# Variance as squares on ScalarE, a two-piece output projection and a new order in a hybrid block of two attentions and two feed-forwards

## The reference

```python
x = x + attn_a(layernorm(x))     # one head of 128
x = x + ffn(layernorm(x))        # 512 -> 512, weight dequantised from 4 bits
x = x + attn_b(layernorm(x))     # 32 heads of 16, rotary, causal
x = x + ffn(layernorm(x))        # the same weights again

def layernorm(x, eps=1e-5):
    return (x - mean(x)) / sqrt(var(x) + eps)
def attn_b(x):
    q, k, v = x @ wq, x @ wk, x @ wv          # 512x512 each
    q, k = rotary(q), rotary(k)
    return softmax(causal(q @ k.T / 4)) @ v @ wo
```

## Time and profile before

| | us |
|---|---|
| median of three runs | 279.03 |
| profiled execution, own time | 280.3 |
| its span, first to last instruction | 278.3 |
| TensorE busy | 259.2 |
| VectorE busy | 227.9 |
| GpSimd busy | 180.8 |
| ScalarE busy | 145.0 |

### The profile page before, as it was taken

The page is one execution under the profiler, slowest core; times in us unless marked ns, Lnnn a source line. Parts: engine busy times, 40 slices in busy tenths (PEclk is TensorE's granted clock), DMA queues, the critical chain, the costliest instruction groups (busy, mean ns, idle before and its releaser), DMA issues.

```text
span 278.3 us, 6590 instructions
## 1 busy us (share of the span) xinstructions
PE 259.2 (93%) x2358; PEld 212.6 (76%) x2358; DVE 227.9 (82%) x390; ACT 145.0 (52%) x231; POOL 180.8 (65%) x233
## 2 busy tenths in 40 slices
PE   7489999999999999899899999899999799997984
PEld 2389887797979888687887987877778667785642
DVE  3772869879699999989998999988999888838656
ACT  3768885743465354548225459336265464273140
POOL 5556989999783947746589777477649630573060
PEclk9999999999999999999999999999999999999999
DMA  7995090202454445315423633043454431121002
GB/s 221 324 389 199 1 246 22 75 2 84 144 151 124 126 132 148 96 58 149 115 71 104 189 104 103 24 131 102 124 160 114 132 91 50 41 78 40 0 15 98
DMA packets 50903, 31.85 MB, mean 114 GB/s; under 512 B 5368, under 2 KB 46008, under 8 KB 50872
## 3 DMA queue, kind: packets, MB, share of 16 engines
q1 hardware_dynamic: 50872, 31.44, 37.2%
HBM read 22.91 MB, written 8.39 MB: 112 GB/s over the span
## 4 chain that ended last, share of the span: by engine, by line
PE 73%; SPq 8%; DMA 7%; DVE 6%; issue 3%; ACT 1%; POOL 1%; DVEq 0%; POOLq 0%
PE psum L838 12%; PE psum L839 11%; PE psum L840 11%; SPq L467 6%; PE psum L1001 5%; PE psum L922 5%; PE psum L923 5%; PE psum L864 4%; PE psum L987 4%; PE psum L966 4%; PE psum L912 3%; DMA QK<-mrow 2%; PE psum L964 2%; PE psum L989 2%; DMA QK<-qk_parts 2%
## 5 line engine op out<-in xcount | busy, mean ns | idle before, releaser
L556 POOL TENSOR_SCALAR_AFFINE_SELECT E<-E 128x512 f32<-128x512 f32 x64 | 40.1, 652 | 37.1 <-ACT E L682 37.0
L682 ACT ACTIVATE E<-psum 128x1536 f32<-128x1536 f32 x32 | 46.4, 1450 | 31.9 <-PE psum L989 27.5
L794 DVE TENSOR_REDUCE nmax<-psum 128x4 f32<-128x512 f32 (+1 forms) x64 | 59.5, 943 | 2.5 <-PE psum L966 2.3
L838 PE MATMUL psum<-XT_lo,wb_hi 128*128 128x256 f32 x128 | 38.6, 301 | 0.0
L585 ACT ACTIVATE XN<-X,offset,rstd 128x512 f32<-128x512 f32 x32 | 25.5, 806 | 20.5 <-POOL offset L518 20.5
L839 PE MATMUL psum<-XT_hi,wb_lo 128*128 128x256 f32 x128 | 36.1, 282 | 0.0
L840 PE MATMUL psum<-XT_hi,wb_hi 128*128 128x256 f32 x128 | 36.1, 282 | 0.0
L563 ACT ACTIVATE parts<-SH 128x512 bf16<-128x512 f32 x32 | 19.8, 626 | 27.8 <-POOL SH L545 14.3
L838 PE MATMUL psum<-wb_lo,XT_hi 128*128 128x256 f32 (+1 forms) x96 | 31.9, 333 | 0.5 <-DVE inv_o L808 0.3
L966 PE MATMUL psum<-QK 128*128 128x128 bf16 x256 | 29.7, 220 | 1.4 <-DMA QK<-qk_parts 1.4
L840 PE MATMUL psum<-wb_hi,XT_hi 128*128 128x256 f32 (+1 forms) x96 | 30.6, 318 | 0.0
(11 more groups left out here) (101 smaller groups left out, 676.6 us busy)
## 6 DMA issues: line engine op xcount, KB each, us to landing
QK<-qk_parts SPq DMA_DIRECT2D x192, 64.0 KB
qk_parts<-parts SPq DMA_DIRECT2D x16, 384.0 KB, 2.8
X<-L_attn_a_x SPq DMA_DIRECT2D x8, 256.0 KB, 5.7
out<-X SPq DMA_DIRECT2D x8, 256.0 KB, 2.1
wb_raw<-L_attn_b_wk SPq DMA_DIRECT2D x1, 1024.0 KB, 9.0
wb_raw<-L_attn_b_wq SPq DMA_DIRECT2D x1, 1024.0 KB, 11.4
wb_raw<-L_attn_b_wv SPq DMA_DIRECT2D x1, 1024.0 KB, 12.4
QK<-mask_rows SPq DMA_DIRECT2D x8, 128.0 KB
```

The source lines that it names most:

```text
L556: last = nc.gpsimd.affine_select(out=e, in_=e, compare_op=ALU.is_ge, fill=0.0, base=0, pattern=[[0, GH], [1, P]], channel_multiplier=-1)
L682: nc.scalar.activation(E[:, n % 2], bank(3, 3), ACT.Exp, scale=float(HD) ** -0.5).then_inc(done[k], 1)
L794: nc.vector.tensor_reduce(nmax[:, u % 2, g::NG, t], (bank(1, 2) if t else bank(0)).rearrange("p (h k) -> p h k", h=GH), AX, ALU.max, negat ...
L838: nc.tensor.matmul(out_, stat[0], mov[1], start=first, stop=False)
```

## The change

- `LN` stays for the eight tiles of the first norm and the last batch's two tiles of the fourth. For the other 22 tiles the addition that makes X (`WD`, `FD`, `OD`) also sums its row (`accum_out`), and a new ScalarE step `SQ` makes the squares of sum minus 512 x, with their sum. `RS` scales either kind of statistics; two of its operations on a tensor of constants become operations with immediates, and the first two do not wait for each other.
- `WO` goes in two pieces, the first three 128s of the contraction (nine matmuls) and the last one (three); `DH` and `DL` too.
- For the last batch's last feed-forward `F`, `FD` and `OS` go in two halves of 256 columns.
- `NX` divides in place and `NB` reads it with strides; the buffer `TN` is gone.
- Several waits of TensorE that an earlier wait covers are gone.
- `PLAN` is written in a new order, with three `KP` steps (14, 5 and 5 matmuls) in place of four (14, 4, 5 and 7).

The diff without the list and without the dropped waits:

```diff
+PIECES = (slice(0, KT - 1), slice(KT - 1, KT))
+        def row_sums(s, b, t):
+            return {} if ("LN", s, b, t) in nth else {"accum_out": mv[:, (s - 1) * B + b, t, 0:1]}
...
+                    if ("SQ", s, b, 0) in nth:
+                        pool.wait_ge(done["SQ"], last_of(*[("SQ", s, b, t) for t in range(NT)[ts]]))
+                        one, square = 1.0 / C, float(C) ** -3
+                    else:
+                        pool.wait_ge(done["LN"], last_of(*[("LN", s, b, t) for t in range(NT)[ts]]))
+                        one, square = 1.0, 1.0
+                    nc.gpsimd.tensor_scalar(mv[:, sl, ts, 0], mv[:, sl, ts, 0], -one, None, ALU.mult).then_inc(pool_link, 1)
+                    links[0] += 1
+                    link(nc.gpsimd.tensor_scalar(mv[:, sl, ts, 1], mv[:, sl, ts, 1], square, EPS, ALU.mult, ALU.add))
...
+                elif k == "SQ":
+                    s, b, t = st[1:]
+                    act.wait_ge(done[made_x(s, b, t)[0]], upto(*made_x(s, b, t)))
+                    if nth[st]:
+                        act.wait_ge(done["SQ"], nth[st])
+                    moments = mv[:, (s - 1) * B + b, t]
+                    nc.scalar.activation(squares[:], X[:, b, t], ACT.Square, bias=moments[:, 0:1], scale=-float(C),
+                                         accum_out=moments[:, 1:2]).then_inc(done[k], 1)
...
-                    act.wait_ge(done["NB"], last_of(*[("NB", KT * b + m) for m in range(KT)]))
+                    act.wait_ge(done["NB"], last_of(*[("NB", KT * b + m) for m in range(KT)[PIECES[piece]]]))
...
-                    nc.vector.tensor_tensor(X[:, b, t], X[:, b, t], prod, ALU.add).then_inc(done[k], 1)
+                    if s == 2:
+                        last = nc.vector.scalar_tensor_tensor(X[:, b, t], X[:, b, t], 1.0, prod, ALU.mult, ALU.add,
+                                                              **row_sums(3, b, t))
+                    else:
+                        last = nc.vector.tensor_tensor(X[:, b, t, cols], X[:, b, t, cols], prod, ALU.add)
+                    last.then_inc(done[k], 1)
...
-                    nc.vector.tensor_tensor(X[:, b, t], X[:, b, t], bank(bank_of["WO", b, t]), ALU.add
-                                            ).then_inc(done[k], 1)
+                    nc.vector.scalar_tensor_tensor(X[:, b, t], X[:, b, t], 1.0, bank(bank_of["WO", b, t, 0]), ALU.mult,
+                                                   ALU.add, **row_sums(4, b, t)).then_inc(done[k], 1)
...
-                    nc.vector.tensor_tensor(TN[:].rearrange("p (i g d) -> p i g d", g=NG, d=HD), tr[:, :, :, 0:HD],
+                    nc.vector.tensor_tensor(tr, tr,
...
-                    nc.vector.transpose(O[:, m], TN[:]).then_inc(done[k], 1)
+                    nc.vector.transpose(O[:, m], TR[:].rearrange("p (g i d) -> p i g d", g=NG, d=2 * HD)[:, :, :, 0:HD]
+                                        ).then_inc(done[k], 1)
...
-                    for kt in range(KT):
+                    for kt in range(KT)[PIECES[piece]]:
                         last = three_pass(ps, [xt[:, slot, kt, tok] for xt in (XT_hi, XT_lo)],
                                           [w[:, 3, kt] for w in (wb_hi, wb_lo)], kt == 0, kt == KT - 1)
```

More of the change, by code:

```diff
@@ L239, in bank_turns @@
             continue
-        if k not in READ_BY or (k in PAIRS and st[2]):
+        if k not in READ_BY or (k in PAIRS and st[2]) or (k == "WO" and st[3]):
             continue
@@ L388, in xt_half, with output_part, columns @@
             return xt[:, xt_of[st], :, t * P:(t + 1) * P]
+        def output_part(xt, b, t, piece):
+            return xt[:, xt_of["DH", b, t, piece], PIECES[piece], t * P:(t + 1) * P]
+        def columns(st, at):
+            return slice(st[at] * S, (st[at] + 1) * S) if len(st) > at else slice(0, C)
         part_of = (slice(0, 2 * DA), slice(2 * DA, 3 * DA))
@@ L477, in _ @@
                 elif k == "OS":
-                    b, t = st[1:]
-                    sp.wait_ge(done["FD"], upto("FD", 4, b, t))
-                    sp.dma_start(out_v[b, t], X[:, b, t]).then_inc(out_done, 16)
-            sp.wait_ge(out_done, 16 * B * NT)
+                    b, t = st[1:3]
+                    sp.wait_ge(done["FD"], upto("FD", 4, *st[1:]))
+                    sp.dma_start(out_v[b, t][:, columns(st, 3)], X[:, b, t, columns(st, 3)]).then_inc(out_done, 16)
+            sp.wait_ge(out_done, 16 * count["OS"])
         @block.gpsimd
@@ L751, in _ @@
                     nc.vector.scalar_tensor_tensor(X[:, b, t], bank(bank_of["WA", b, t]), inv_a[:, b % 2, t:t + 1],
-                                                   X[:, b, t], ALU.mult, ALU.add).then_inc(done[k], 1)
+                                                   X[:, b, t], ALU.mult, ALU.add, **row_sums(2, b, t)).then_inc(done[k], 1)
                 elif k == "FS":
@@ L822, in _ @@
                     dve.wait_ge(done["NX"], upto("NX", u))
-                    if m == 0 and b:
-                        dve.wait_ge(done["DL"], last_of(*[("DL", b - 1, t) for t in range(NT)]))
-                    nc.vector.transpose(O[:, m], TN[:]).then_inc(done[k], 1)
+                    if m in (0, KT - 1) and b:
+                        dve.wait_ge(done["DL"], last_of(*[("DL", b - 1, t, int(m > 0)) for t in range(NT)]))
+                    nc.vector.transpose(O[:, m], TR[:].rearrange("p (g i d) -> p i g d", g=NG, d=2 * HD)[:, :, :, 0:HD]
+                                        ).then_inc(done[k], 1)
         @block.tensor
@@ L858, in _ @@
                 elif k == "T":
-                    pe.wait_ge(consts_ready, 2)
                     no = ("NO", *st[1:])
@@ L919, in _ @@
                         pe.wait_ge(done["WC"], KT)
-                    ps = take(st)
+                    ps = take(st)[:, 0:cols.stop - cols.start]
                     for kt in range(KT):
-                        nc.tensor.matmul(ps, XT_lo[:, slot, kt, tok], wf[:, kt], start=kt == 0, stop=False)
-                        last = nc.tensor.matmul(ps, XT_hi[:, slot, kt, tok], wf[:, kt], start=False, stop=kt == KT - 1)
+                        nc.tensor.matmul(ps, XT_lo[:, slot, kt, tok], wf[:, kt, cols], start=kt == 0, stop=False)
+                        last = nc.tensor.matmul(ps, XT_hi[:, slot, kt, tok], wf[:, kt, cols], start=False,
+                                                stop=kt == KT - 1)
                     last.then_inc(done[k], 1)
@@ L995, in _ @@
                     pe.wait_ge(done["MK"], upto("MK", u, g))
-                    pe.wait_ge(done["VV"], upto("VV", u // 2))
+                    if u % 2 == 0 and g == 0:
+                        pe.wait_ge(done["VV"], upto("VV", u // 2))
                     ps = (bank(bank_of["PV", u, 0]) if g else take(st))[:, g * S:(g + 1) * S]
```

86 lines of the change are left out of this document (42 added, 44 removed), and 257 rows, old and new, of the table PLAN.

## The result

The kernel after takes 278.06 us, median of 22 runs (276.35 to 280.67), against 279.6 us for the kernel before in the same comparison (22 runs, 278.41 to 280.96). The ratio is 0.993, with a 95% interval of 0.991 to 0.995: 2.0 us faster (0.7% of 279.6; the medians lie 1.5 us apart), where 6.5 us were forecast. Two of the 22 runs, at 280.51 and 280.67 us, are more than 1.5% above the fastest and are left out of the ratio. The profiled execution took 278.1 us, with a span of 276.4 us, against 280.3 and 278.3 before.

The account below looks back on a forecast made before the run. TensorE was taken to bound the long middle, chains of dependent steps the head and tail. Gains of 1.4 + 3.0 + 0.8 + 1.3 = 6.5 us against the median 279.03 gave 272.5 us, range 269.0 to 278.5.

Parts of the forecast that it names:

- The middle: 30 to 250 us: with VectorE relieved and the new order, 3.0 of TensorE's 6.1 us idle go; bounds nothing and 6.1.
- the middle gives nothing: Rival: TensorE's middle waits are for DMAs and their issuing queue, not VectorE; only 3.5 us won, 275.5 us; chance 0.12.
- The other half of the argument: Middle, unit 12: 60 matmuls instead of 36 stand between transposed maxima (MT) and the product needing them (ST).
- The head: Start to about 29 us: first QK matmul 2.8 us sooner, at about 11.9; net gain 1.4 us, bounds 0 and 2.8.
- The end of the heads: 250 to 256.3 us: F 4,1,1 before the last units and moved transposes win 0.8 of 1.2 us idle.
- The tail: Last 22 us: projection in pieces and halved last feed-forward end 1.3 us sooner; fillers spend the early win; bounds 0.5 and 3.5.
- The prices: Assumed instruction costs: squares with accumulator read 0.99 us each, row-sum additions 0.1 us more each, halved copies some 0.1 us.
- The lower bound of the relief: VectorE's work was to fall by 10 to 19 us, 14 taken; the lower bound is the 10.
- ScalarE as the relay: Rival: squares waiting in ScalarE's in-order queue hold exponentials and copies behind them, up to 281 to 282 us; chance 0.16.
- seven exposed squares: In the ScalarE rival: each exposed square costs 0.99 us or more; from 7 of 22 the whole gain is gone.
- only eats the gain: Milder part of the ScalarE relay rival: 277.6 to 280.4 us; chance 0.07 of its 0.16.
- The clock: Rival in the tail: clock drops to 1.2 GHz, four half products (3.8 us) take twice as long, 276.3 us; chance 0.04.

Follow-up runs that it names:

- experiment 2: No statistics for 22 tiles: old order against the kernel before, 279.55 us, ratio 1.001; kernel after without its squares, 276.86 us, ratio 0.991.
- the relieved run, the run without statistics: Old order with no statistics for 22 tiles (constant variance), in-place division and row sums in, against the kernel before: 279.55 us, ratio 1.001.
- experiment 1: Parts alone: new order with VectorE's statistics 285.72 us; squares in the old order 285.29 us; new tail in the old order 287.48 us.
- late pieces: Kernel after with both first pieces of the last batch copied and subtracted no earlier than the last piece: 285.51 us, ratio 1.021.
- both fillers: Kernel after plus ten filler matmuls in the head's pause and five in the tail's: 277.04 us, ratio 0.989.
- experiment 4: Kernel after with the last batch's first pieces late, 285.51 us, ratio 1.021; kernel after without the tail's ten fillers, 278.74 us, ratio 0.997.
- experiment 3: Old order with squares on ScalarE, one copy of transposed exponentials moved ahead of two squares: 284.19 us, ratio 1.015; unmoved 285.29 us.
- the run without fillers: Kernel after without the ten filler matmuls of the tail: 278.74 us, ratio 0.997.
- both fillers and both moves: Kernel after with fillers in its two longest pauses, plus TensorE work moved into two waits of the middle: 280.48 us, ratio 1.002.

## Why the forecast was wrong

Of the 6.5 us, 1.9 came in the spans. The missing 4.6 us are about 2.3 in the middle and 2.0 in the head.

**The middle (3.0 us forecast, 0.7 us less idle).** This is the step that failed first: that VectorE, at 192.6 of 220 us, delays what it hands on, so that half of TensorE's 6.1 us of idle time would go with its relief. In the old order the relief, without its price on ScalarE, is worth 0.0 us (ratio 1.001, experiment 2). A mean load told me that VectorE was late, but not where: at the longest wait of the old order the relief took nothing away, and VectorE is as full there as before (6.94 of 7.00 us). Issue and transfer, 4.1 us, take the rest. The rival "the middle gives nothing" (275.5 us) had this nearly right, though not its reason: the queue that issues was not in the way at 217 us, the two transfers of unit 12 were issued 0.07 us behind VectorE's result in the relieved run. The other half of the argument, the 60 matmuls between MT and ST of unit 12, did remove that wait; but 1.0 us for normalised rows, 0.8 for nmax and a wait of 1.3 for stacked parts (0.9 the longest before) stand in the new order. What the relief does is carry the new order (7.6 us, experiment 1), and that order only makes good what its own positions ask of VectorE.

**The head (1.4 us forecast).** The working was right to 0.2 us for the first product, and from there to 29 us the longest wait is indeed 0.3 us. It put at nothing what lies ahead of that product: one pause of 2.4 us, made of two of 1.5, since the second tile's transposes came earlier and the third normalisation did not. The pause costs nothing by the chain, but in the profiled execution the granted clock fell to 0.50 behind it, 1.46 us at QV, which eats the forecast's 1.4. An estimate of the whole from TensorE's busy time up to 30 us (23.59 before; 25.38 after, of which 1.46 are the fall and 0.91 the slower fillers at the start) has TensorE 0.6 us behind in work. By the same reckoning the executions with late pieces and with both fillers, which kept their clock, are 1.1 to 1.2 us ahead, so the term itself was near.

**The end of the heads (0.8 us forecast).** Idle time there is 0.56 us (6.30 - 5.74), 0.6 less than before. About right in size. But F 4,1,1 was not moved forward: it stood ahead of unit 13's PV and now stands behind unit 14's scores, so this busy time came into the stretch from the middle.

**The tail (1.3 us forecast, 1.3 measured).** Right, and with its parts: 3.67 us to the first addition for 3.6, the second tile's transposes 13.3 us behind VectorE's transposition as before, and the last addition's end 1.1 us nearer to it (274.16 - 255.73 = 18.43, before 275.89 - 256.36 = 19.53). Wrong was to call the fillers a loss (experiment 4).

**The prices.** Squares take 719 ns and 193 ns for their accumulator read, 0.91 us for the 0.99 taken. Additions with a row sum were bounded by 0 and 0.28 us and taken as 0.1. The addition itself costs nothing more (688 ns for 687), and there is a second instruction of 82 ns, as the Trainium skill, "VectorE: DVE Perf Modes", section "Two Vector instructions with no wait between them", says:

```profile
L803 DVE SCALAR_TENSOR_TENSOR X<-X,psum 128x512 f32<-128x512 f32 x8 | 5.5, 688 | 0.3
...
L803 DVE DVE_READ_ACCUMULATOR X<-X,psum 128x1 f32 x8 | 0.7, 82 | 0.0
```

Two pieces of a remainder take 627 and 467 ns for one of 769, so 0.33 us more a tile, where some 0.1 was taken; the two copies, 518 and 302 ns for 621, cost 0.20. The lower bound of the relief was added up wrong as well: its own terms give 9 us, not 10. The division in place looks cheaper by the mean, 421 ns for 641, but not by the median (min/median/max, before and after):

```profile
L816 DVE TENSOR_TENSOR TN<-TR,inv_o x16: 406/421/2492, 112.2 to 257.4; 128x256 f32<-128x256 f32 x16
```

```profile
L855 DVE TENSOR_TENSOR TR<-TR,inv_o x16: 404/422/466, 112.4 to 256.8; 128x256 f32<-128x256 f32 x16
```

A few long ones make the mean of before (the longest 2.49 us), and in place in the old order, in the run without statistics, there are such too (mean 624 ns). So 3.6 of VectorE's 18.4 us are not the change of form; what makes these long ones was not looked for.

**The rivals.** ScalarE as the relay showed up where I changed one part alone (experiment 3). In the real change the squares cost 0.5 us by the ratios and 1.2 at the medians (experiment 2), not the price of seven exposed squares. The measured median lies in the band that was given to "only eats the gain", but that is not what ate it. The clock was a rival with a chance of 0.04, placed in the tail; 15 of 22 runs show some fall, the profiled one in the head, and the tail lost its clock in the run without fillers. In runs without a fall the change is worth 2.7 us: 276.87 against 279.6, the median of those 45 of the 59 runs of the kernel before in the experiments that have a mean clock of 0.996 or more. Most of what is then missing to 6.5 is the middle.

## What to carry to other kernels

A mean load of 88% does not say where an engine is late: before crediting its relief, take the largest waits, follow each back, and see whether the work that goes away stands ahead of the instruction that is late. A hand-written order belongs to its own set of operations; moving one step into a gap of 1 to 2 us moved the wait elsewhere or doubled it in both tries here. And where steps come earlier, ask what TensorE does behind them: two pauses of 1.5 us became one of 2.4, which costs nothing by the chain and 1.2 us or more when the clock falls. With filler matmuls in the two longest pauses all six runs kept their clock.

## What the runs showed of the hardware

The clock does not fall every time: behind the same pause of 2.3 to 2.4 us it went to 0.50 for about 3.3 us in three profiled executions and stayed at 1.00 in two, and the runs of one kernel fall into groups 1.2 us and more apart for it. In a kernel with such a pause the median tells how often the clock fell, so I would read the mean clock of each run beside its time. What decides between the two I could not see.

A granted clock of 1.00 did not mean full speed at the start of the program: the first 14 fillers took 6.07 us in the kernel after and 4.82 in the run with both fillers and both moves, 0.43 and 0.34 us each, with 1.00 shown all the while, and 0.22 us each in the tail.
